# Conditioned attention layers: y of the first layer is turned by VectorE and through DRAM instead of by TensorE, and other work changes engines with it

## What the kernel computes

```
# first layer: full attention, then conditioned normalisation
xn = layer_norm(x);  q, k, v = xn @ q_w + q_b, xn @ k_w + k_b, xn @ v_w + v_b
att = softmax(einsum('bnhl,bmhl->bnmh', q, k) + (1 - mask) * -1e6, axis=2)
y = einsum('bnmh,bmhl->bnhl', att, v * mask)
scale, shift = split(silu(cond) @ emb_w + emb_b)
x = x + silu(layer_norm(y) * (1 + scale) + shift) @ out_w + out_b
# second layer: linear attention, the same conditioned block after it
q = softmax(q over a head's features);  k = softmax(k over positions, masked)
y = q @ (k^T v) per head;  x = x + silu(layer_norm(y) * (1 + scale) + shift) @ W + b
```

## Time and profile before

| | |
|---|---|
| median of 3 runs | 869.07 us (866.77 to 870.33) |
| the profiled execution's own time | 869.6 us |
| its span, first to last instruction | 867.8 us |
| TensorE matmuls busy | 832.3 us, 96% of the span |
| VectorE busy | 773.2 us, 89% |
| ScalarE busy | 679.0 us, 78% |
| GpSimd busy | 679.9 us, 78% |
| mean granted clock of TensorE | 0.994 |

### The profile page before, as it was taken

The page is one execution under the profiler, slowest core; times in us unless marked ns, Lnnn a source line. Parts: engine busy times, 40 slices in busy tenths (PEclk is TensorE's granted clock), DMA queues, the critical chain, the costliest instruction groups (busy, mean ns, idle before and its releaser), DMA issues.

```text
span 867.8 us, 23658 instructions
## 1 busy us (share of the span) xinstructions
PE 832.3 (96%) x8092; PEld 686.9 (79%) x8092; DVE 773.2 (89%) x1590; ACT 679.0 (78%) x1208; POOL 679.9 (78%) x1165
## 2 busy tenths in 40 slices
PE   4999999999999999999999988999999999999996
PEld 4777777777777777777777656899999999999996
DVE  6689999999998999999998967899999999999976
ACT  2247777777777777777778796899999999999975
POOL 3375878878888888888786337899999999999965
PEclk9899999999999999999999999999999999999999
DMA  8854665565656565655654424345454444444311
GB/s 258 263 175 165 198 219 187 207 209 191 220 183 212 179 222 181 221 196 196 219 178 164 142 64 107 96 126 144 152 149 143 136 142 140 138 150 141 116 31 62
DMA packets 129847, 143.69 MB, mean 166 GB/s; under 512 B 13312, under 2 KB 85984, under 8 KB 129600
## 3 DMA queue, kind: packets, MB, share of 16 engines
q1 hardware_dynamic: 129728, 142.19, 50.5%
HBM read 49.50 MB, written 38.11 MB: 101 GB/s over the span
## 4 chain that ended last, share of the span: by engine, by line
PE 77%; DVE 13%; issue 6%; POOL 1%; ACT 1%; SPq 1%; DMA 0%; DVEq 0%; ACTq 0%; POOLq 0%
PE psY L1721 12%; PE psX L1600 11%; PE psT L1600 10%; PE psM L1600 10%; DVE sb_cm L1158 6%; PE psT L1700 5%; PE psY L1600 5%; PE psT L1679 4%; PE psT L1883 3%; PE psY L1836 3%; PE psT L1611 3%; PE psM L1700 3%; PE psY L1746 2%; DVE sb_xF L1172 2%; PE psM L1679 2%
## 5 line engine op out<-in xcount | busy, mean ns | idle before, releaser
L1158 DVE TENSOR_REDUCE sb_cm<-psT 128x4 f32<-128x1024 f32 x168 | 202.8, 1213 | 20.5 <-PE psT L1700 20.3
L741 ACT ACTIVATE sb_P<-psT 128x1024 f32<-128x1024 f32 x176 | 177.8, 1026 | 42.6 <-PE psY L1721 23.5
L1721 PE MATMUL psY<-sb_P,sb_Vp 128*17 128x256 f32 x2048 | 129.4, 381 | 1.9 <-DVE sb_yr L1193 1.2
L1158 DVE TENSOR_REDUCE sb_cm<-psM 128x4 f32<-128x1024 f32 x88 | 106.7, 1213 | 11.5 <-PE psM L1700 11.5
L741 ACT ACTIVATE sb_P<-psM 128x1024 f32<-128x1024 f32 x80 | 82.0, 1025 | 21.6 <-PE psY L1721 11.7
L1600 PE MATMUL psX<-sb_xT,sb_W0h 128*128 128x256 f32 x488 | 93.6, 294 | 0.0
L1721 PEld LDWEIGHTS psY<-sb_P,sb_Vp 128*17 128x17 f32 x2048 | 50.3, 97 | 46.8 <-DVE sb_yr L1193 1.9
L521 POOL TENSOR_TENSOR sb_qp<-sb_qp 128x512 fp32r<-128x512 f32 x64 | 82.3, 1285 | 5.3
L1700 PE MATMUL psT<-sb_Ks,sb_Qs 64*128 64x256 f32 x672 | 76.6, 310 | 2.6 <-DVE sb_cm L1158 2.5
L1679 PE MATMUL psT<-sb_Qs,sb_Ks 64*128 64x256 f32 x704 | 75.5, 298 | 1.6 <-ACT sb_P L741 1.4
L1600 PEld LDWEIGHTS psX<-sb_xT,sb_W0h 128*128 128x128 f32 x488 | 71.4, 192 | 4.6 <-ACT sb_qp L764 0.2
(11 more groups left out here) (215 smaller groups left out, 2553.4 us busy)
## 6 DMA issues: line engine op xcount, KB each, us to landing
sb_Qs<-sb_qp SPq DMA_DIRECT2D x96, 256.0 KB
sb_Ks<-sb_qp SPq DMA_DIRECT2D x96, 256.0 KB
sb_xt<-in_x SPq DMA_DIRECT2D x32, 256.0 KB, 3.4
y_normed<-sb_Yn SPq DMA_DIRECT2D x32, 256.0 KB, 2.7
sb_u<-y_normed SPq DMA_DIRECT2D x128, 64.0 KB, 2.6
out<-sb_v SPq DMA_DIRECT2D x31, 256.0 KB, 2.4
x_biased<-sb_xo SPq DMA_DIRECT2D x28, 256.0 KB, 2.3
sb_u<-x_biased SPq DMA_DIRECT2D x28, 256.0 KB, 3.3
```

Source lines behind the costliest of these rows:

```text
L741: a.activation(P[G % 4][:, :], pairs[place["S", n, g][0]][:, :], ACT.Exp).then_inc(s_ex, 1)
L1158: v.tensor_reduce(cm[n % 2][:, 4 * j:4 * j + 4], scores, AX.X, ALU.max, negate=True).then_inc(s_mx, 1)
L1721: ins = pe.matmul(psY[32 * j:32 * j + 17, y0:y0 + T], Vp[n % RING][:, m, 4 * gr + j, :], Pj[:, c0:c0 + 256], start=(m == 0), stop=(m == 1))
```

## The change

- **y is turned without TensorE.** For batches 0 to 27 (TAIL), VectorE transposes each half of psY in blocks of 32 by 32 straight from PSUM into a part of the tile yT (`yblock`), takes the reciprocal of the sums from there (`yroot`), GpSimd multiplies (`share`), SP stores the result to a DRAM tensor (`qstore`) and loads it back with four DMAs that exchange the blocks (`qload`, runs of 64 elements), and VectorE computes the statistics from there (`ylanded`). TensorE's transposes, ScalarE's copies and VectorE's `divide` stay for the last four batches only. The heads are dealt to the value products in another order, and the columns of q and k with them (`by_d`), so that the blocks fall in place. ynorm comes a turn later.
- **The masks of the values** (`vmask`) move from GpSimd to ScalarE, between the first and second exponential.
- **The statistics of x** of batches 10 and up (SUMMED) are made by ScalarE: two sums with an accumulator after the second exponential (`xsum`), the mean by GpSimd (`xmean`), and two sums of squares at the end of the turn (`xsquares`).
- **x is made a turn ahead**: from turn 6 on its load, its block loads and its transpose come earlier against the turn that uses it.
- The small transpose of the column maxima moves from before the second q/k projection to between the last two score groups.

```diff
+            def qstore(n):
+                sp.wait_ge(s_yq, 2 * n + 2)
+                sp.dma_start(qd[n], yq).then_inc(s_qd, 16)
+            def qload(n):
+                sp.wait_ge(s_qd, 16 * (n + 1))
+                if n >= 2:
+                    sp.wait_ge(s_y, n - 1)
+                by_block = qd[n].rearrange("(j s) (k b e) -> b s k j e", j=4, k=2, b=4)
+                tile = yrs[n % 2].rearrange("p k (j e) -> p k j e", j=4)
+                for b in range(4):
+                    sp.dma_start(tile[32 * b:32 * b + 32], by_block[b]).then_inc(s_yl[n % 2], 16)
...
+            def xmean(n):
+                g.wait_ge(s_sx, 2 * (n - SUMMED) + 2)
+                g.wait_ge(s_xn, n)
+                g.tensor_scalar(nm[:, 0:2], sx[:, 0, :], -1.0 / D, 0.0, ALU.mult, ALU.add).then_inc(s_rs, 1)
...
+            def share(n, half):
+                g.wait_ge(s_yi, 2 * n + half + 1)
+                if half == 0 and n >= 1:
+                    g.wait_ge(s_qd, 16 * n)
+                root = ri[:, half, :].rearrange("p (g b a) -> p g b a", g=2, a=1).to_broadcast([128, 2, 8, DH])
+                g.tensor_tensor(yq.rearrange("p (b g d) -> p g b d", b=8, g=4)[:, 2 * half:2 * half + 2],
+                                yG[half][:, :, :, 0:DH], root, ALU.mult).then_inc(s_yq, 1)
...
             for t in range(B):
                 if t >= BY_BLOCK:
                     xlow(t)
-                if BIASED <= t + 1 < B:
+                if ok(t - 5):
+                    share(t - 5, 1)
+                if t >= BY_BLOCK and ok(t + 2):
+                    xnorm(t + 2)
+                if BIASED <= t + 1 <= BY_BLOCK:
                     xbias(t + 1)
-                for_later(t)
-                if ok(t - 5):
-                    ynorm(t - 5)
+                if ok(t - 6):
+                    ynorm(t - 6)
+                if ok(t - 4):
+                    share(t - 4, 0)
+                if SUMMED <= t + 3 < B:
+                    xmean(t + 3)
                 if ok(t - 2):
                     csplit(t - 2)
-                if ok(t - 1):
-                    vmask(t - 1)
...
+            def xsum(n):
...
+                for k in range(2):
+                    a.activation(xn[:, k, :], xt[n % 2][:, k, :], ACT.Identity, accum_out=sx[:, 0, k:k + 1])\
+                        .then_inc(s_sx, 1)
+            def xsquares(n):
...
+                for k in range(2):
+                    a.activation(xn[:, k, :], xt[n % 2][:, k, :], ACT.Square, bias=nm[:, k:k + 1],
+                                 accum_out=sx[:, 1, k:k + 1]).then_inc(s_sq, 1)
...
                 exps(t, 0)
-                if ok(t - 4):
-                    yturn(t - 4, 0)
+                if ok(t - 1):
+                    vmask(t - 1)
                 exps(t, 1)
+                if SUMMED <= t + 3 < B:
+                    xsum(t + 3)
                 exps(t, 2)
...
+            def yblock(n, half):
+                v.wait_ge(s_pv, 4 * n + 2 * half + 2)
+                if n >= 1:
+                    v.wait_ge(s_yq, 2 * n - 1 + half)
+                v.transpose(yG[half].rearrange("p g b c -> p (g b) c"), psY[:, :].rearrange("p (x c) -> p x c", c=32))\
+                    .then_inc(s_yg, 1)
+            def yroot(n, half):
+                v.wait_ge(s_yg, 2 * n + half + 1)
+                v.reciprocal(ri[:, half, :], yG[half].rearrange("p g b c -> p (g b) c")[:, :, 16]).then_inc(s_yi, 1)
...
-                elif gr == 0 and n >= 1:
-                    pe.wait_ge(s_yd, 8 * n - 2)
                 elif gr == 0:
-                    pe.wait_ge(s_cs, 2)
+                    pe.wait_ge(s_yg, 2 * n)
+                    pe.wait_ge(s_cs, n + 2)
                 elif gr == 2:
-                    pe.wait_ge(s_ye, 2 * n + 1)
+                    pe.wait_ge(s_yg, 2 * n + 1)
```

More of the change, by code:

```diff
@@ L144, in bass_cond_seq_kernel @@
         xT1 = [xT[:, :, :], xT2[:, :, :]]
+        blocked, moved = (t[:, :, :].rearrange("p q t -> p (q t)") for t in yT)
+        yG = [blocked[:, 512 * i:512 * i + 512].rearrange("p (g b c) -> p g b c", g=2, b=8) for i in range(2)]
+        yq = moved[:, 0:512]
+        yrs = [yr[:, :, :], moved[:, 512:1024].rearrange("p (k d) -> p k d", k=2)]
         ph = sb("ph", [128, 2])
@@ L236, in bass_cond_seq_kernel @@
             sem(f"s_{n}") for n in ("sT", "ex", "pv", "ye", "yt", "yd", "yr", "y"))
+        s_yg, s_yi, s_yq, s_qd, s_ys = (sem(f"s_{n}") for n in ("yg", "yi", "yq", "qd", "ys"))
+        s_sx, s_sq = sem("s_sx"), sem("s_sq")
+        s_yl = [sem(f"s_yl{i}") for i in range(2)]
         s_yo = [sem(f"s_yo{i}") for i in range(2)]
@@ L424, in _ @@
                     xload(t + 3)
-                if ok(t + 2) and t + 2 > BY_BLOCK:
+                if t + 1 == BY_BLOCK:
                     nstore(t + 2)
@@ L436, in _ @@
                     nstore(t + 2)
-                if ok(t + 2) and t + 2 >= BY_BLOCK:
+                if BY_BLOCK - 2 <= t < BY_BLOCK:
                     nblocks(t + 2)
+                if t + 1 == BY_BLOCK:
+                    xstore(t + 2)
+                    xload(t + 4)
                 if t + 1 < RING:
@@ L772, in cturned, with vmask @@
                 a.activation(ct[:, :].bitcast(F32R), psY[0:64, 0:128], ACT.Identity).then_inc(s_cs, 1)
+            def xsum(n):
+                a.wait_ge(s_x[n % 2], landed(n, 2))
+                a.wait_ge(s_xtr, BY_BLOCK)
+                if n > SUMMED:
+                    a.wait_ge(s_rs, 3 * n - 2)
+                    a.wait_ge(s_sq, 2 * (n - SUMMED))
+                for k in range(2):
+                    a.activation(xn[:, k, :], xt[n % 2][:, k, :], ACT.Identity, accum_out=sx[:, 0, k:k + 1])\
+                        .then_inc(s_sx, 1)
+            def xsquares(n):
+                a.wait_ge(s_rs, 3 * n + 1)
+                a.wait_ge(s_sx, 2 * (n - SUMMED) + 2)
+                for k in range(2):
+                    a.activation(xn[:, k, :], xt[n % 2][:, k, :], ACT.Square, bias=nm[:, k:k + 1],
+                                 accum_out=sx[:, 1, k:k + 1]).then_inc(s_sq, 1)
+            def vmask(n):
+                a.wait_ge(s_vb, n + 1)
+                if n >= RING:
+                    a.wait_ge(s_pv, 4 * (n - RING) + 4)
+                for k in range(2):
+                    ins = a.activation(Vp[n % RING][:, k, :, 0:16], vb[:, k, :].rearrange("p (h d) -> p h d", d=DH),
+                                       ACT.Identity, scale=mT[:, k, n:n + 1])
+                ins.then_inc(s_v, 1)
             def yturn(n, half):
                 a.wait_ge(s_pv, 4 * n + 2 * half + 2)
-                if n >= 2:
-                    a.wait_ge(s_yt, 2 * n - 2)
+                if n == TAIL:
+                    a.wait_ge(s_yq, 2 * TAIL)
+                elif n == TAIL + 1:
+                    a.wait_ge(s_y, TAIL)
+                else:
+                    a.wait_ge(s_yt, 2 * (n - TAIL) - 2)
                 a.activation(yT[n % 2][:, 2 * half:2 * half + 2, :], psY[:, :].rearrange("p (g t) -> p g t", g=2),
@@ L1450, in _ @@
                     first_turn()
+                if ok(t - 4):
+                    yblock(t - 4, 0)
                 maxima(t, 2)
+                if t > BY_BLOCK and ok(t + 1):
+                    xturn(t + 1)
+                if ok(t - 4):
+                    yroot(t - 4, 0)
                 if 1 <= t < BY_BLOCK - 1:
                     stats(t + 1, 0)
[L1454 removed]
+                elif t == BY_BLOCK - 1:
                     stats(t + 2, 0)
[L1456 to L1457 removed]
                 if t == 1:
```

216 lines of the change are left out of this document (119 added, 97 removed).

## The result

The changed kernel takes **919.67 us** (median of 4 runs, 916.31 to 921.24) against 868.64 us for the kernel before, measured beside it. The ratio is 1.0588, with a 95% interval of 1.0563 to 1.0613: 51 us slower, where 853 us had been forecast. What happened is the mechanism of rival 4 (SP's queue becomes the bound), which had a chance of 0.10 and was priced at 876.

A forecast was written before the change was run, and what follows sets the result against it. TensorE was taken to bound the first layer, VectorE close behind. Gains of 13.4 (turns 8 to 28), 2.8 (29 to 31) and 1.0 (4 to 7), less 0.5 at hand-over: 869.6 - 16.7 = 853 us, range 847 to 859.

The forecast's parts named there:

- rival 4: SP's queue becomes the bound at y's four block reloads: loop 16.4, about 876 us, chance 0.10.
- The loop is 9.22 + 0.4 + 2.0 + 2.0 to 2.7 = 13.6 to 14.3: just covered: SP's queue per turn: existing issues, added store, four reloads and the store's landing, claimed to fit within the 14.3 turn.
- the 3.05: SP's time for four x block loads in one traced turn, called rare against the usual 2.00.
- its 10.27: SP's back-to-back issues from zero rows to y store in the kernel before, including 3.05 for four x block loads.
- TensorE's saving of 1.21: Removing y's transposes from TensorE, 0.53 + 0.68 us per turn.
- 14.3 was forecast: Turn length in the middle, down from 14.94: TensorE's 13.93 plus a 0.37 wait.
- The small transpose's place: On TensorE, moving it between two score groups was to cost 0.2 us per turn for an extra switch.
- the wait for the fourth exponential: TensorE waits for scratch that ScalarE's fourth exponential frees before a score group, 0.37 us per turn.
- the early turns: Turns 4 to 7, with x statistics crowded on VectorE, were to gain 1 us in all, none to 3.
- rival 3: GpSimd bounds if its multiplications are slow, 1.47 or 1.2 us apiece: 858 to 868 us, chance 0.08.
- Rival 2: ScalarE takes the gain back: accumulator reads and masks cost more, turn 15.0, 867 us, chance 0.17.
- Rival 1: No new wait for the fourth exponential, TensorE alone bounds: 846 us, chance 0.15.

The follow-up runs named there:

- e2: Changed kernel without y's store and reload through DRAM, so its blocks are not exchanged and part of the computation is missing: 861.62 us, ratio 0.9931.
- e10: e9 with the small transpose of the column maxima back before the second q/k projection, exchange of blocks still left out: 852.72 us, ratio 0.9828.
- e9: e2 with ScalarE's sums of x moved behind the sixth exponential and GpSimd's mean of x later: 857.48 us, ratio 0.9881.
- e18: Changed kernel with a second tile for the divided y, so GpSimd need not wait for the previous turn's store: 919.04 us, ratio 1.0589.
- e14: Changed kernel with y's reload after x's load, zero and mask rows before x's block reload, x sums later, small transpose earlier: 900.15 us, ratio 1.0350.
- e20: e15 with a second tile for the divided y: 873.17 us, ratio 1.0065.
- e15: e14 with one of y's four reloads issued by ScalarE behind the fifth exponential: 888.71 us, ratio 1.0230.
- e25: e20 with the normalised y's store behind x's load and a second y reload issued by ScalarE: 872.19 us, ratio 1.0047.
- e4: Kernel before plus an unused store and four reloads of the previous turn's block, so SP does not stand still: 878.31 us, ratio 1.0117.

## Why the prediction was wrong

**The step that failed is SP's queue**, the sentence "The loop is 9.22 + 0.4 + 2.0 + 2.0 to 2.7 = 13.6 to 14.3: just covered". Measured are 15.6 and 16.8 in the rows shown and 16.65 on average. Its parts:

- The 9.22 run from the start of the zero rows to the start of y's store, so the store's own issue, 0.5 there and 0.60 with its gap of 0.1 now, was counted nowhere. This was an error of reading: a loop must be summed from a start to the same start. (The store of x is missing too, but costs nothing, as it is issued while y's store lands.)
- The four reloads take 2.66 with their gap, not 2.0: 0.61 each, where x's four take 1.81 in the same turn, 0.45 each; on average, with long issues, 2.97. The nearest row was of another shape, 512-byte runs. The Trainium skill, "DMA: Bandwidth & Descriptors", "Specifications", asks for 512 bytes or more for line rate. Of a longer landing, which the prediction drew from it, the trace shows little (2.4 us against 2.2 for x's blocks of the same 64 KB); the larger difference is in the issue.
- The store lands after 2.57 and 2.93 in the rows shown, 3.0 at the median, where 2.0 to 2.7 had been taken from quieter queues. The landing is counted from the start of the store's issue (301.10 to 303.67), so the 0.4 for that issue was counted twice.
- Long issues: in a full queue an issue now and then takes 1.2 us or more instead of 0.6 (311.12, the 2.81 of x's four loads). One such row, the 3.05, was in the profile and was set aside as rare. Such issues (over 0.9 us) come 0.3 times a turn in the kernel before, 0.8 in e2, whose queue has slack too, and 1.1 in the changed kernel; what brings them on is open. A queue with 4 us of idle time a turn absorbs it; a full one pays every time.

On average the loop went from 13.97 (its middle) to 16.65 by 0.70 for y's store, 0.97 for the reloads (0.31 of it long issues), 0.28 for the landing (3.03 instead of 2.35 and 0.4), and 0.73 for the rest, mostly long issues. Rival 4 named the right place, and its sum of 16.4 was near, but by luck in part: its 10.27 leaves out y's store as the 9.22 does, and all eight loads being long makes up for it. It was priced halfway, at 15.4, with a slack that would last five turns; no such stretch of short turns is in the trace.

**What held, without the trip.** TensorE's saving of 1.21 is right: e10, with neither the wait nor the move, has turns of 14.0 to 14.1 us for the most part, and 14.94 - 1.21 + 0.24 for its new wait is 13.97. In e2 the turn is 14.48 where 14.3 was forecast. The small transpose's place cost 0.3 to 0.4, not 0.2, and the wait for the fourth exponential 0.2, not 0.37; with these the turn would be 14.2 to 14.3, so that 0.2 of e2's turn is not accounted for. Without the trip the change takes 861.6 us, not 853. Of the 8.6 us between, about 4 are 21 turns at 14.48 instead of 14.3. Another 3.5 lie behind the last v bias: from there to the end e2 takes 389.2 us (859.9 - 470.7), the kernel before 385.2 (867.8 - 482.6), where the sum had 0.5. And the early turns, which were to gain 1 us, lose 1 (77.6 us for the five from the first v bias out of psX, against 76.5). The prices: block transpose 0.71 whole against 0.62 to 0.70; mask 0.50 whole, 0.90 the pair, as taken; sums of x 0.41 and 0.19 for the read, as taken; division 0.62 against 0.737, so GpSimd's work did not bound the changed kernel, and rival 3 is out. Rival 2 is out by e9, which puts ScalarE's part at 0.2 a turn. Rival 1's condition, no wait for the fourth exponential, is met in e9 and e10 alone.

The Trainium skill, "VectorE: DVE Perf Modes", "Rules for kernel authors", would have kept the transposes on TensorE. Its verdict, no gain, was nearer to the result, and the limit to blocks of 32 by 32 that the prediction noted beside it is what cost: the work of the transposes fits on VectorE (e2 and e10, which leave out the exchange of blocks, gain 0.7 and 1.7%), but such a transpose leaves blocks to be exchanged between partitions, and by way of DRAM that took 58 us.

## What to carry to other kernels

Sum an in-order queue like an engine: every issue from one start to the same start of the next turn, with the landing that it waits for, and compare that with the turn; when it comes close (13.6 to 14.3 beside 14.3 here), count the long issues too. A store and its reload on one queue needed about 3 us of other issues between them here, and moving one trip uncovered the next, so look at all round trips of the queue at once. A large wait on an engine that is not in the ring is worth nothing (e18), and the same edits can gain in one ring and lose in another (e10, e14): first find the ring, then edit.

## What was not expected of the hardware

- What the issue of a DMA costs SP's queue differs by its shape: 0.32 to 0.60 for a store of 256 KB in rows of 2 KB, 0.43 to 0.45 for a load of 64 KB in runs of 512 bytes, 0.61 for one in runs of 256 bytes, 0.60 for the tiles of q and k. The same store of x takes 0.32 in the kernel before, whose queue has idle time, and 0.46 or 0.66 in the full queue.
- ScalarE issues such a load for much the same price, 0.56 us (e20's chain). Taking one off SP gained 11 and 7 us (e15, e20) and a second one 5 (e25), where 21 x 0.6 is 12.6.
- Five more issues a turn, with 34,500 more packets (129,847 before, 164,344 with the trip) and a DMA share of 0.71 instead of 0.59, cost the kernel before 10 us (e4), though no engine waits for the data. Its queue is full then (0.3 us idle a turn); issues and packets are not told apart.
